# Gated cross attention on one core: X G1^T, X W and the last two products moved into separate Strassen phases, with spills to DRAM

## The reference

```python
memory_proj = einsum('bme,de->bmd', memory, W_mem)            # P = C W^T
scores = einsum('bnd,bmd->bnm', hidden_states, memory_proj) / sqrt(D)
attn = softmax(scores, axis=-1)                               # A
memory_context = einsum('bnm,bmd->bnd', attn, memory_proj)    # M = A P
gate_input = concatenate([hidden_states, memory_context], axis=-1)
gate = sigmoid(einsum('bnf,df->bnd', gate_input, W_gate) + b_gate)
fused = hidden_states + gate * memory_context
return rmsnorm(fused, norm_w)
```

## Time and profile before

| | |
|---|---|
| median of 3 runs | 1047.63 us (1046.73 to 1047.76) |
| span of the profiled execution | 1045.4 us |
| PE busy | 1001.6 us, 4992 matmuls |
| DVE busy | 763.8 us |
| ACT busy | 281.4 us |
| POOL busy | 89.7 us |
| HBM read, written | 63.96 MB, 16.78 MB |

### The profile page before, as it was taken

The page is one execution under the profiler, slowest core; times in us unless marked ns, Lnnn a source line. Parts: engine busy times, 40 slices in busy tenths (PEclk is TensorE's granted clock), DMA queues, the critical chain, the costliest instruction groups (busy, mean ns, idle before and its releaser), DMA issues.

```text
span 1045.4 us, 13484 instructions
## 1 busy us (share of the span) xinstructions
PE 1001.6 (96%) x4992; PEld 837.6 (80%) x4992; DVE 763.8 (73%) x1277; ACT 281.4 (27%) x418; POOL 89.7 (9%) x97
## 2 busy tenths in 40 slices
PE   6997999999999999999999999999999999999996
PEld 5986788888878888887878888887888888788885
DVE  4996686776778677677768767676867767787774
ACT  4441223222221322223222222223232132222222
POOL 2240001010100101010010101000010100001010
PEclk9998999999999999999999999999999999999998
DMA  7961113112021312202131221212122131213101
GB/s 210 244 183 28 61 41 101 60 61 100 20 80 60 100 60 76 84 21 80 62 98 60 80 80 36 85 59 82 60 82 79 40 102 39 80 60 100 61 10 72
DMA packets 72895, 80.97 MB, mean 77 GB/s; under 512 B 5936, under 2 KB 59184, under 8 KB 72880
## 3 DMA queue, kind: packets, MB, share of 16 engines
q1 hardware_dynamic: 72880, 80.76, 25.1%
HBM read 63.96 MB, written 16.78 MB: 77 GB/s over the span
## 4 chain that ended last, share of the span: by engine, by line
PE 80%; DVE 14%; ACT 3%; issue 2%; SPq 1%; DMA 0%; POOL 0%; DVEq 0%; POOLq 0%; ACTq 0%
PE psum L717 27%; PE psum L718 26%; PE psum L720 26%; DVE at L564 7%; DVE pt L556 1%; DVE at_l L505 1%; ACT prob L450 1%; DVE stat L607 1%; ACT at_h L400 1%; DVE prob L614 1%; DVE g_l L505 0%; ACT g_h L400 0%; DMA ring<-in_L_xattn_W_gate 0%; SPq L195 0%; SPq L200 0%
## 5 line engine op out<-in xcount | busy, mean ns | idle before, releaser
L556 DVE STREAM_TRANSPOSE pt<-psum 32x256 f32<-32x256 f32 x512 | 228.2, 446 | 45.5 <-ACT p_h L400 38.8
L717 PE MATMUL psum<-g_h,xt_h 128*128 128x512 f32 x512 | 202.2, 395 | 0.9 <-DVE p_l L505 0.9
L718 PE MATMUL psum<-g_l,xt_h 128*128 128x512 f32 x512 | 202.1, 395 | 0.0
L720 PE MATMUL psum<-g_h,xt_l 128*128 128x512 f32 x512 | 160.6, 395 | 0.0
L717 PEld LDWEIGHTS psum<-g_h,xt_h 128*128 128x128 f32 x512 | 96.5, 188 | 23.1 <-DVE p_l L505 1.3
L720 PEld LDWEIGHTS psum<-g_h,xt_l 128*128 128x128 f32 x512 | 96.5, 188 | 22.7
L718 PEld LDWEIGHTS psum<-g_l,xt_h 128*128 128x128 f32 x512 | 96.6, 189 | 21.7
L717 PE MATMUL psum<-wt_h,ct_h 128*128 128x512 f32 x256 | 101.2, 395 | 0.0
L717 PE MATMUL psum<-k_h,ctt_h 128*128 128x512 f32 x256 | 100.9, 394 | 0.0
L718 PE MATMUL psum<-wt_l,ct_h 128*128 128x512 f32 x256 | 100.9, 394 | 0.0
L718 PE MATMUL psum<-k_l,ctt_h 128*128 128x512 f32 x256 | 100.9, 394 | 0.0
(11 more groups left out here) (103 smaller groups left out, 1715.3 us busy)
## 6 DMA issues: line engine op xcount, KB each, us to landing
xrow<-in_x SPq DMA_DIRECT2D x32, 512.0 KB, 3.7
out<-xrow SPq DMA_DIRECT2D x31, 512.0 KB, 2.6
stage<-in_x SPq DMA_DIRECT2D x64, 128.0 KB, 2.8
stage<-in_ctx SPq DMA_DIRECT2D x16, 512.0 KB, 3.4
gate<-in_x SPq DMA_DIRECT2D x60, 128.0 KB, 2.7
gate<-in_ctx SPq DMA_DIRECT2D x60, 128.0 KB, 2.6
ring<-in_L_xattn_W_gate SPq DMA_DIRECT2D x44, 128.0 KB, 3.5
ring<-in_L_xattn_W_mem SPq DMA_DIRECT2D x28, 128.0 KB, 3.5
```

Of the source, the lines that this page charges most:

```text
L556: last = nc.vector.transpose(pt32[BLK * q:BLK * q + BLK, :, col:col + BLK], tile[BLK * qm:BLK * qm + BLK, :, q, :])
L717: nc.tensor.matmul(tile, ah, mh, start=start and i == 0, stop=False)
L718: nc.tensor.matmul(tile, ah, ml, start=False, stop=False)
L720: last[t] = nc.tensor.matmul(tile, al, mh, start=False, stop=stop and i == len(pairs) - 1)
```

## The change

The one loop becomes three phases over all batches, and the host hands over x, C, W and G1 in the order in which the partitions want them (x and C both plain and transposed, G2 transposed), so VectorE's block transposes all go. The result is written in a partition-major order, too.

- Fold: K as before, in 192 matmuls of 512 columns; K is stored to DRAM (`kd`).
- Phase X G1^T (called gx below): for each batch a Strassen-Winograd product of 2 x 2 blocks, 7 products of 12 matmuls of 512 columns where 8 would be needed. The sums of blocks of x are made on VectorE (`x_sums`, 4 for each batch), the 7 blocks are cut (`x_cut_high`, `x_cut`), and each of the 7 results is added on VectorE into z (`gx_out`), which goes to DRAM (`zd`). The 7 blocks of G1 are summed and cut once.
- Phase Y = X W (two batches at a time, 8 steps): 7 products of 24 matmuls of 256 columns, X as the moving operand, results to DRAM (`yd`). The sums of blocks of W are made on GpSimd, those of x on VectorE.
- Attention: for each batch S = Y C^T (24 of 256 columns), softmax, A turned by four TensorE transposes with an identity matrix, T = C^T A^T (24 of 256), and a Strassen product of T with [W^T, K], 7 x 2 products of 6 matmuls of 512 columns (`mem_gate`), whose left half is M and whose right half is added to z. Scores, turn and context of batch b+1 are placed between the products of batch b.

The diff, cut to its core. It replaces the whole body; lines of the same name keep their meaning.

```diff
--- before.py
+++ after.py
...
-        wt_h, wt_l = (const(f"wt_{s}", [PART, KE, D], F32R) for s in "hl")
-        k_h, k_l = (const(f"k_{s}", [PART, KE, D], F32R) for s in "hl")
-        g1_h = const("g1_h", [PART, KD, D], F32R)
...
+        kd = nc.dram_tensor("k_spill", [PART, KE, D], F32).ap()
+        yd = nc.dram_tensor("y_spill", [B, PART, KE, N], F32).ap()
+        zd = nc.dram_tensor("z_spill", [B, PART, NB, D], F32).ap()
...
+            for i in range(2):
+                sp.wait_ge(k_act, 2 * i + 2)
+                sp.wait_ge(k_dve, 2 * i + 2)
+                sp.dma_start(kd[:, 2 * i:2 * i + 2, :], k_out[i][:, :, :]).then_inc(k_stored, DMA)
+            sp.wait_ge(k_stored, 2 * DMA)
+            sp.dma_start(xs_raw[1][:, :, :], xt[1]).then_inc(x_in[1], DMA)
...
+            for b in range(B):
+                if b + 2 < B:
+                    sp.wait_ge(gx_mm, P7 * (b + 1))
+                    sp.dma_start(xs_raw[b % 2][:, :, :], xt[b + 2]).then_inc(x_in[b % 2], DMA)
...
+                sp.wait_ge(gx_z, P7 * (b + 1))
+                sp.dma_start(zd[b], z[b % 2][:, :, :]).then_inc(z_stored[b % 2], DMA)
...
+                    sp.wait_ge(y_mm, P7 * s)
+                    if s + 1 < SB:
+                        load_y(s + 1)
+                    else:
+                        load_attention(sp)
+                sp.wait_ge(y_copied, 4 * s + 4)
+                sp.wait_ge(y_added, 3 * s + 3)
+                for i in range(2):
+                    sp.dma_start(yd[2 * s + i], y[s % 2][:, i, :, :]).then_inc(y_stored[s % 2], DMA)
...
+                pool.tensor_tensor(r[T1][:, :, :], r[T3][:, :, :], r[0][:, :, :], ALU.subtract).then_inc(wb_sum, 1)
+                pool.wait_ge(wb_sum, 4 * m + 1)
...
+                act.wait_ge(wb_sum, 8)
+                act.wait_ge(y_mm, Y_LAST - P7 + 3 + n // 2 if n < 8 else Y_LAST)
+                copy(wb_h[m][i][:, :, :], wb_raw[m][i][:, :, :]).then_inc(wb_high, 1)
+            def first_high():
+                act.wait_ge(y_mm, Y_LAST - P7)
+                act.wait_ge(yt_in, DMA)
+                copy(yt_h[:, :, :], yt_raw[:, :, :]).then_inc(yt_high, 1)
+                act.wait_ge(ct_in, DMA)
+                copy(ct_h[:, :, :], ct_raw[:, :, :]).then_inc(ct_high, 1)
+                act.wait_ge(c_in, DMA)
+                copy(c_h[:, :, :], c_raw[:, :, :]).then_inc(c_high, 1)
...
+            def mem_copy(b, i):
+                dst, bk = {0: (mem[:, 0, HALF[0]], 0), 2: (mem[:, 0, HALF[1]], 0), 3: (mem[:, 1, HALF[1]], 1),
...
+            for b in range(B):
+                mem_copy(b, 0)
...
+                else:
+                    tanh(b - 1, 1)
+                    square(b - 1, 1)
+                if b + 1 < B:
+                    exps(b + 1)
+                mem_copy(b, 2)
+                if b + 2 < B:
+                    act.wait_ge(yt_in, DMA * (b + 3))
...
+                mem_copy(b, 3)
+                if b + 2 < B:
+                    act.wait_ge(ct_in, DMA * (b + 3))
+                    copy(ct_h[:, :, :], ct_raw[:, :, :]).then_inc(ct_high, 1)
+                if b + 1 < B:
+                    at_cut_high(b + 1)
+                tanh(b, 0)
+                if b + 1 < B:
+                    t_cuts_high(b + 1)
+                square(b, 0)
+                mem_copy(b, 6)
+                if b + 2 < B:
+                    act.wait_ge(c_in, DMA * (b + 3))
+                    copy(c_h[:, :, :], c_raw[:, :, :]).then_inc(c_high, 1)
+            tanh(B - 1, 1)
+            square(B - 1, 1)
...
+            for k in range(3):
+                fold_low_part(k)
+            fold_low_part(3)
+            g1_t1()
+            g1_cut(0)
+            fold_low_part(4)
+            g1_t2()
+            g1_cut(T1)
+            g1_cut(B22)
+            fold_low_part(5)
+            g1_t4()
+            g1_cut(1)
+            g1_cut(T2)
+            fold_low_part(6)
+            g1_cut(T3)
+            g1_cut(T4)
+            fold_low_part(7)
...
+            for n in range(GX_LAST):
+                b, i = n // P7, n % P7
+                gx_out(b, i)
+                if b + 1 < B:
+                    if i == 0:
+                        x_sums(b + 1, 0)
+                        x_sums(b + 1, 1)
+                    elif i in (1, 2):
+                        x_sums(b + 1, i + 1)
+                if n + XH < GX_LAST:
+                    x_cut(n + XH)
...
+            for s in range(SB):
+                for i in range(P7):
+                    n = P7 * s + i
+                    if i in (1, 4, 5):
+                        y_add(s, i)
+                    if s + 1 < SB:
+                        if i == 3:
+                            y_sums(s + 1, 0)
+                            y_sums(s + 1, 1)
+                        elif i == 4:
+                            y_sums(s + 1, 2)
+                            y_sums(s + 1, 3)
+                    if n + YH < Y_LAST:
+                        y_cut(n + YH)
...
+                    if s == SB - 1:
+                        if i == 1:
+                            first_low()
...
+            t_first(0)
+            wb_cut(8)
+            wb_cut(9)
+            t_second(0)
+            for w in range(10, 2 * P7):
+                wb_cut(w)
+            for b in range(B):
+                z_out(b, 0)
+                if b >= 1:
+                    fuse(b - 1, 1)
+                mem_add(b, 1)
+                z_out(b, 1)
+                if b == 0:
...
+                if b + 1 < B:
+                    maxima(b + 1)
+                if b >= 1:
+                    scale_rows(b - 1, 1)
+                if b + 1 < B:
+                    probs(b + 1)
+                z_out(b, 2)
+                z_out(b, 3)
+                if b + 2 < B:
+                    dve.wait_ge(yt_high, b + 3)
+                    low(yt_l[:, :, :], yt_raw[:, :, :], yt_h[:, :, :]).then_inc(yt_low, 1)
+                mem_add(b, 4)
+                z_out(b, 4)
+                if b + 1 < B:
+                    at_cut(b + 1)
+                if b + 2 < B:
+                    dve.wait_ge(ct_high, b + 3)
+                    low(ct_l[:, :, :], ct_raw[:, :, :], ct_h[:, :, :]).then_inc(ct_low, 1)
+                mem_add(b, 5)
+                z_out(b, 5)
+                if b + 1 < B:
+                    t_first(b + 1)
+                fuse(b, 0)
+                if b + 1 < B:
+                    t_second(b + 1)
+                z_out(b, 6)
+                scale_rows(b, 0)
+            fuse(B - 1, 1)
+            scale_rows(B - 1, 1)
...
+            for k in range(KD):
+                pe.wait_ge(fold_low, 2 * k + 2)
+                for e in range(KE):
+                    cols = slice(PART * e, PART * e + PART)
+                    for h in range(2):
+                        last = three(bank(2 * e + h), wn_h[:, k, cols], wn_l[:, k, cols], g2_h[k % 3][:, HALF[h]],
...
+            for n in range(GX_LAST):
+                b, i = n // P7, n % P7
+                b1, b2, b3 = gx_banks(b)
+                bk = (b1, b2, b1, b3, b1, b3, b1)[i]
+                if b == 0:
+                    pe.wait_ge(g1_low, g1_pos[i] + 1)
+                pe.wait_ge(x_low, n + 1)
+                if b < 2 and i in (0, 1, 3):
+                    pe.wait_ge((k_act, k_dve)[bk % 2], bk // 2 + 1)
+                elif i == 0:
+                    pe.wait_ge(gx_z, P7 * (b - 1))
+                if i in (2, 4, 5, 6):
+                    pe.wait_ge(gx_z, P7 * b + {2: 1, 4: 3, 5: 4, 6: 5}[i])
+                lo = x_block(b % 2, i)[1]
+                for k in range(4):
+                    last = three(bank(bk), xh[n % XH][:, k, :], lo[:, k, :], g1_h[i][:, k, :], g1_l[i][:, k, :],
+                                 k == 0 and i in (0, 1, 3), k == 3)
+                last.then_inc(gx_mm, 1)
...
+                b1, b2 = y_banks(s)
+                bk = (b1, b2, b1, b2, b1, b2, b1)[i]
+                pe.wait_ge(y_low, n + 1)
+                if s == 0:
...
+                wh, wl = w_block(i)
+                lo = y_block(s % 2, i)[1]
+                for et in range(2):
+                    cols = slice(PART * et, PART * et + PART)
+                    for k in range(4):
+                        last = three(psum[:, bk, N * et:N * et + N], wh[:, k, cols], wl[:, k, cols],
+                                     yh[n % YH][:, k, :], lo[:, k, :], et == 0 and k == 0 and i in (0, 1, 3), k == 3)
+                last.then_inc(y_mm, 1)
+                if s == SB - 1:
+                    if i == 2:
+                        pe.wait_ge(gx_z, GX_LAST)
+                        scores(0)
+                    elif i == 4:
+                        turn_probs(0)
+                    elif i == 5:
+                        context(0)
...
+            def mem_gate(b, i):
+                slot = t_slot(b, i)
+                pe.wait_ge(t_low, 5 * b + (1, 2, 4, 4, 5, 5, 3)[i])
+                for m in range(2):
...
+                        if i == 0 and b >= 1:
```

(37 more changed lines are left out.)

1398 lines of the change are left out of this document (755 added, 643 removed).

## The result

The changed kernel takes **1119.69 us** (median of 4 runs, 1115.8 to 1121.35), the kernel before 1047.2 on the same chip: a ratio of 1.0688, 95% interval 1.0668 to 1.0709. It is 72 us slower. The forecast was 1150 in a range of 1070 to 1190, slower with a chance of 0.85: the sign is right and the time is 30 us (2.7%) too long. The profiled execution took 1121.35 with a span of 1119.6.

A forecast was written before the change was run, and what follows sets the result against it. The prediction took TensorE to bound the kernel before; phase terms of 652.5 us, 14 attention batches at 33.0 (462) and a tail of 33 made a span of 1147.5, with 2.2 more a median of 1150, range 1070 to 1190.

The forecast's parts named there:

- fold ends: Set-up phase making K: start at 8.5 us, VectorE's last cut at 56, the last eight products done at 62.
- first batch of gx: First X G1^T batch: 31 us, 19.6 of matmuls, a stall of 8.3 for the second x, 2.9 for the clock.
- into Y, idle: Seam from gx to Y: 13 us, first cut ready 8.4 after gx ends, clock 2.9, contention 2.
- Y, steps 1 to 7: X W phase: 157 us, from steps of 20.2, 28.2 and five of 21.1, plus 3 for GpSimd's sums.
- step 8, first attention batch: Y's last step and the first attention batch: 95 us, 52 of it matmuls, late scores, clock losses 3.
- 14 attention batches: Steady attention loop: 33.0 us each against 25.8 of matmuls, 4.6 idle for ScalarE's late copy, 2.5 clock; 462 in all.
- Rival 4: All stages: matmul paces 10% shorter than the rows, about 75 us less, giving 1075; chance 0.05.
- Rival 2: Attention batch's edge: small operations on T overlap, hiding the hand-over, TensorE stays the bound; about 1020 us; chance 0.13.
- rival 3: Loads of x in gx, Y and step 8: 1 MB needs 7.5 us, not 5.4, giving 1179; chance 0.07.
- The named cover: In the fifteen further gx batches: slack of 0.9 to 1.6 us for x's landing; every us beyond costs 15.
- Contention with GpSimd: VectorE slowed beside GpSimd's sums: 2 us into Y, 3 more in Y, up to 10.
- rival 1: Attention gaps and seams: the chain holds but the clock doesn't fall, giving 1101 us; chance 0.20.

The follow-up runs named there:

- e1: The changed kernel with ScalarE's copy of the last memory product, which frees bank 0, moved ahead of the norm's square: 1075.05 us (1.0268).
- e3: The changed kernel with 12 further matmuls of 512 columns, results unused, in the idle gap after each attention batch's last product: 1093.12 us (1.0435).
- e10: e8 with the second x's sums made after product 4 of the first gx batch and Y's x loads issued before the store of z[14]: 1016.39 us (0.9710).
- e9: e8 with GpSimd's last W sum and four low parts of W put behind VectorE's first two cuts of x for Y: 1026.97 us (0.9821).
- e4: The changed kernel with GpSimd's sums of [W^T, K] spread one at a time over later products of Y: 1108.65 us (1.0593).
- e5: e4 with SP issuing the next x before the blocks of W^T and K: 1102.43 us (1.0526).
- e2: e1 with VectorE also making the T sums and the last z sum before the gated sum: 1070.93 us (1.0233).
- e6: The changed kernel with the memory copy right after T's small cuts, the last z add before T's second cuts and gated sum, C's cut moved: 1061.63 us (1.0141).
- e8: The changed kernel with the edits of e5 and e6, plus reordered cuts and first scores in Y's step 8 and first attention batch: 1028.57 us (0.9823).
- e12: e9 and e10 together, with ScalarE making the last two W sums' high parts behind the first Y operand's high part: 1015.87 us (0.9707).

## Why the prediction came out as it did

The sum of the prediction against landmarks of the trace. Each part is a difference of starts on TensorE's timeline:

| part | predicted | measured |
|---|---|---|
| fold ends | 62 | 61.8 |
| first batch of gx | 31 | 27.8 |
| 15 batches of gx | 294 | 292.4 |
| into Y, idle | 13 with clock | 13.9 |
| Y, steps 1 to 7 | 157 | 161.4 |
| step 8, first attention batch | 95.5 | 90.4 |
| 14 attention batches | 462 | 440.0 |
| tail | 33 | 31.9 |
| span | 1147.5 | 1119.6 |

**The attention batch is the step that was mis-sized: 22 of the 28 us.** The mechanism was right to the instruction: ScalarE's copy behind the square, the square behind VectorE's gated sum, that behind seven operations on T; e1 shows it. The chain from the end of the context was put at 7.3 us and took 6.9 (638.06 to 644.98), so the gap is 4.0 and not 4.6. The clock behind it was put at 2.5 and costs 1.83 (e3). The matmuls themselves were put at 25.8 and are 25.6 here (31.43 - 4.01 - 1.83). 14 x 1.57 us is the error. The clock term is a little the larger part of it: of its bounds, 1.6 to 2.9, I took a value near the upper one, and the measurement lies near the lower.

**The fold.** It ends where it was put, and VectorE's last cut lets the last product start at 56.3 (56 said). On the way the terms differ: TensorE starts at 7.2 and not at 8.5, and waits 4.3 us in the middle, with half clock behind that.

**The work.** The pace held: a gx batch takes 19.5 us (19.6), six matmuls of 512 columns 1.36 to 1.40. Rival 4 falls; its price was also put too low, since 10% of 671 + 253 us of matmuls is 92 and not 75. Rival 2 falls too: the chain at the edge fits in the product only after its order is changed. The prediction took its 216 and 109 ns from the Trainium skill, TensorE: Matmul & The Clock Gate (Back-to-back issue gap). That section gives them as the gap of matmuls issued by themselves, and 131 ns at 512 columns for a stream with a weight load for each. The rows here, 227 to 233 ns, agree with neither.

**x lands late, and it costs nothing.** 1 MB takes 6.5 us to land in gx, not 5.4, and 7.0 and 9.4 in Y, where 7.5 was rival 3's condition. The named cover, 0.9 to 1.6 us, took nearly all of it in gx: the eight waits for z beside the first add up to 2.1 us and are at most 0.5. So rival 3 was half right on the landing and wrong on the price.

**First batch of gx.** The second x landed at 74.2 and not at 77, since K's stores were done at 69.4 and not at 72; the seven operations behind it took the 4.3 that was said. The stall is 5.75 instead of 8.3. e10 confirms the cause: moved sums, no stall. (In the earlier trace rows the clock falls at 90.2 and 110.7, not at 90.4 and 110.85 as the prediction reads it; nothing in the sum changes.)

**Into Y and Y: the sum hides large errors of both signs.** Contention with GpSimd was put at 2 into Y and 3 in Y, "up to 10". It is 7.6 into Y (e9) and about 9 in Y (e4: 4.93 + 4.07), over three times as much in all. The earlier trace rows had the right slowdown, 3.4 for 1.2 us, but I priced it on a few operations, while VectorE has five such operations ahead of Y's first product, with adds of z between them. Each gap also cost its half-clock time: steps 1 and 2 lost 7.6 us to it (60.6 us for 40.3 of matmuls and 12.7 of waits), where 2.9 were put. Against that, the other parts of the wait into Y are 6.3 and not 8.4, and steps 3 to 7 take 20.16 each, without the 0.9 us of waiting each that x was to cost. Step 2's wait for the load order, put at 8, is 7.7 in the trace, but e4 and e5 split it into 4.1 of contention and 3.7 of order: a right number with half the reason. Over the seam and Y together contention and clock took 16 us more than was put and the other terms 11 less; that the sum comes within 5.3 us is luck.

**Step 8 and the first batch.** The first scores waited 9.6 (8.5 said), the second 8.5 (11.7 said), the turn 0.7 (1.4) and the context 2.9 (3). The clock losses, put at 3, are larger: half clock stands from 569.1 to 579.3, 593.0 to 596.4, 603.2 to 606.6 and 613.4 to 623.7, with TensorE at work for about 15 us of it, so some 7.5 us by the estimate above.

**The clock holds (rival 1).** Not in the changed kernel; in the attention loops of e1, e2, e3, e6 and e8 to e12 it does. It goes with the gap, as the earlier trace rows had it: gaps of 1.1 and 1.3 us in each batch leave it at 1.00, gaps of 4.0 us don't. In between both occur. In e8 a gap of 2.0 us at 559.2 is followed by 1.00 for 12 us, and one of 2.1 at 570.9 by half clock from 572.0 to 575.4; in e4 a gap of 2.8 at 42.4 is followed by 1.00, and the like gap at 50.9 by half clock from 51.1 on. So the length of one gap does not settle it there.

Together, e10 and e12 show that the change loses by its seams and the orders of its lists, not by its arithmetic: with the same matmuls it then runs 30 and 31 us faster than the kernel before, of 57 us of work saved by the count.

## What to carry to other kernels

Before adding up a saving in matmuls, list the waits that each new phase boundary and each list order adds, and read what stands ahead of the one short copy that frees the bounding engine's bank: moving 0.6 us of work ahead of a 1.1 us operation, and of the wait of that operation, was worth 45 us here. Price a gap on TensorE twice, as idle time and as half-clock time, and know that two short gaps can be cheaper than one long one. Price each long VectorE operation with two SBUF operands (128x1024 here) at up to nearly three times its length wherever GpSimd's `tensor_tensor` works beside it, and look for where it goes when it is moved.

## What the runs showed of the hardware

A VectorE operation on two tensors of SBUF (128x1024) took 1.21 to 1.23 us alone and mostly 3.05 to 3.43 beside GpSimd's `tensor_tensor` (less, as 2.76 at 393.61 in e8, where GpSimd's operation was nearer its end), while adds with one operand in PSUM kept 0.68 (at 393.01 in e8, GpSimd busy throughout). Where neither was held up before, the one that began second paid: in e2 GpSimd took its usual 2.40, and VectorE, 0.07 us later, 3.41, about its 1.28 and what was left of GpSimd's 2.40. In long runs of both each took some 3.3, GpSimd's too. The Trainium skill says this in SBUF — State Buffer (Who interferes with whom): a two-input VectorE operation and a GpSimd one that reads SBUF contend for one port pair, and the later one blocks until the first is done. The trace agrees: in e2 VectorE's operation ends 1.08 us after GpSimd's, not much less than the 1.28 that it takes alone.

The clock's price per gap: 1.5 (e1) to 1.83 us (e3) for 4.0 us of idle; none for gaps of 1.1 and 1.3 us in each batch, where the granted clock is 1.00 over 360 us.
